# Image and vector field loaded ahead of weights and late gathers, VectorE's first step in an order of its own, attention masks of one head read four times

## What is computed

```python
# image filter, per image o (vf0, vf1: the vector field)
u = sigmoid(o / 0.5); q = 0
for _ in range(10):
    q = max(q - 0.5 * (rowdiff(u) * vf1 + coldiff(u) * vf0), 0)
    Tq = div(vf1 * q, vf0 * q)          # differences the other way
    u = sigmoid((o - Tq) / 0.5)
img = (o - Tq) / 0.5
# text
h = emb[tokens] + positions
for l in range(4):
    h = layernorm(h + attention(h, l)); h = layernorm(h + mlp(h, l))
# fusion on concat(img, h)
mask = (j <= i) & (j > i - 64)          # the same for all 8 heads
h = h + window_attention(layernorm(h), mask)
h = h + spikes(relu(layernorm(h) @ Wfc) ** 2 @ Wproj)
```

## Time and profile before

| | |
|---|---|
| median of 3 runs | 1001.82 us (1001.42 to 1001.96) |
| the profiled execution | 999.17 us, of which the span of its instructions is 997.3 us |
| busy in the span | PE 905.2 us (91%), DVE 834.9 (84%), ACT 699.3 (70%), POOL 122.3 (12%) |
| chain that ended last | DVE 47%, PE 25%, ACT 16%, issue 9%, DMA 2% |
| granted TensorE clock | 0.976 in the mean |

### The profile page before, as it was taken

One profiled execution on the slowest core, in us unless ns is written; L12 is line 12 of the kernel. 1 busy time (PEld: TensorE's weight loads), 2 busy tenths in 40 slices (PEclk: granted clock), 3 DMA queues, 4 the chain that ended last, 5 costly groups with the idle time before them and its releaser, 6 DMA issues.

```text
span 997.3 us, 18874 instructions
## 1 busy us (share of the span) xinstructions
PE 905.2 (91%) x6960; PEld 700.2 (70%) x6960; DVE 834.9 (84%) x1160; ACT 699.3 (70%) x2252; POOL 122.3 (12%) x147
## 2 busy tenths in 40 slices
PE   5489999999999999999999997889998999999997
PEld 4267777777777777777777775767675766667675
DVE  2999999999999999999999998987899599352443
ACT  2666876976877877877876875757767686767842
POOL 6201011011011011101101111101010111000000
PEclk9699999999999999999999999999998999999999
DMA  7311120031010121010220010000001000100000
GB/s 173 113 35 28 66 89 19 22 122 45 18 45 17 32 90 39 17 46 14 70 80 11 17 38 11 12 22 12 27 17 38 17 22 17 44 27 2 17 1 32
DMA packets 24925, 39.00 MB, mean 39 GB/s; under 512 B 4001, under 2 KB 20609, under 8 KB 23553
## 3 DMA queue, kind: packets, MB, share of 16 engines
q1 hardware_dynamic: 24448, 36.74, 11.6%
q0 software_dynamic: 384, 1.05, 0.5%
HBM read 22.21 MB, written 5.24 MB: 28 GB/s over the span
## 4 chain that ended last, share of the span: by engine, by line
DVE 47%; PE 25%; ACT 16%; issue 9%; DMA 2%; POOL 1%; SPq 0%; DVEq 0%; POOLq 0%; ACTq 0%
ACT prob L1086 7%; PE ps_t L849 7%; DVE f L1726 4%; DVE f L1753 4%; PE ps_m L860 4%; DVE f L1748 4%; DVE p L1738 4%; DVE f L1757 4%; DVE neg_max L1762 4%; DVE f L1743 3%; ACT u L1073 3%; DVE f L1721 2%; DVE f L1710 2%; PE ps_s L796 2%; DVE f L1699 2%
## 5 line engine op out<-in xcount | busy, mean ns | idle before, releaser
L1086 ACT ACTIVATE prob<-ps_s,neg_max 128x128 f32<-128x128 f32 x512 | 181.3, 408 | 7.3 <-DVE neg_max L1762 7.3
L1086 ACT ACTIVATION_READ_ACCUMULATOR prob<-ps_s,neg_max 128x1 f32 x512 | 126.6, 249 | 0.0
L655 PE MATMUL ps_t<-w,hidT 128*128 128x256 f32 x512 | 125.7, 383 | 0.0
L1094 ACT ACTIVATE probT<-ps_t 128x512 f32<-128x512 f32 x128 | 81.1, 634 | 44.3 <-PE ps_t L601 28.7
L655 PEld LDWEIGHTS ps_t<-w,hidT 128*128 128x128 f32 x512 | 91.1, 190 | 12.1 <-ACT hidT L1168 3.0
L849 PE MATMUL ps_t<-km,w_fc 128*128 128x384 f32 x256 | 93.9, 503 | 1.0 <-ACT km L1282 1.0
L601 PE MATMUL ps_t<-ident,prob 128*128 128x128 f32 x512 | 81.5, 283 | 12.9 <-ACT prob L1086 6.7
L601 PEld LDWEIGHTS ps_t<-ident,prob 128*128 128x128 f32 x512 | 60.0, 144 | 36.6 <-issue 14.7
L1762 DVE TENSOR_REDUCE neg_max<-ps_s 128x8 f32<-128x1024 f32 x64 | 77.5, 1211 | 4.6 <-PE ps_s L591 4.6
L1341 ACT ACTIVATE prob<-ps_s,neg_max 128x128 f32<-128x128 f32 x192 | 53.8, 376 | 22.6 <-DVE neg_max L1935 22.2
L849 PEld LDWEIGHTS ps_t<-km,w_fc 128*128 128x128 f32 x256 | 47.5, 195 | 26.8 <-issue 3.7
(11 more groups left out here) (179 smaller groups left out, 2038.9 us busy)
## 6 DMA issues: line engine op xcount, KB each, us to landing
w<-in_w SPq DMA_DIRECT2D x8, 1024.0 KB, 5.0
u<-u SPq DMA_DIRECT2D x80, 63.0 KB
p<-p SPq DMA_DIRECT2D x80, 63.0 KB
w_attn<-in_w_attn SPq DMA_DIRECT2D x4, 768.0 KB, 5.4
out<-w SPq DMA_DIRECT2D x7, 384.0 KB, 2.5
o_all<-in_o SPq DMA_DIRECT2D x4, 512.0 KB, 3.7
filtered<-f_out SPq DMA_DIRECT2D x4, 512.0 KB, 3.2
x<-filtered SPq DMA_DIRECT2D x8, 256.0 KB, 2.8
```

What stands on the lines that cost most here:

```text
L655: last = mm(ps_t[:, 0, D * t:D * t + D], hidT[:, m, P * t:P * t + P], w2[:, m], start=False, stop=(m == MC - 1), skip_group_check=True)
L1086: last = A(prob[:, n % 2, hh], ps_s[n % 2][:, hh], ACT.Exp, scale=-1.0, bias=neg_max[:, n % 2, hh:hh + 1], accum_out=den)
L1094: A(probT[:, 4 * half:4 * half + 4].rearrange("p h k -> p (h k)"), ps_t[:, 1], ACT.Copy).then_inc(s["act_pT"], 1)
```

## The change

1. SP issues the image right after the tokens, and the vector field (its column component, `vf[:, 1]`, first, with the semaphore `l_vf`; the row component with `l_vf_rows`) ahead of `w_attn`. Its wait before u<-u of iteration 0 is for eight of POOL's constants (`N_EARLY`) in place of nine.
2. POOL waits for `l_qkv` before it issues the six late gathers. The masks are built for one head: 256 columns to clear in place of 1024, and nine selections on 128 columns in place of 512. The readers take the 128 columns four times, through an access pattern that repeats them.
3. TensorE's 40 transposes at the start wait for eight constants in place of nine. ScalarE's first tanh waits for the constants, its program for `c_pool` at nine as before, and its first key copy for `c_heads` (`head_mask`).
4. VectorE does the first two filter operations before the positions; `head_max(0, 0)`, `(0, 1)` and `(0, 2)` come at other places of `first_step`; `pair_mask` is made between the iterations (`row_pairs`); `normalise(0, 0)` and `(0, 1)` stand before and after `divergence_rows(1)` and not after `divergence_out(1)`.

```diff
             sp.dma_start(tokens[:], d["tokens"]).then_inc(s["l_tok"], 16)
+            load_images(0).then_inc(s["l_img"], 16)
...
             sp.dma_start(pe[:], d["pe"]).then_inc(s["l_pe"], 16)
-            load_images(0).then_inc(s["l_img"], 16)
+            for comp, loaded in ((1, "l_vf"), (0, "l_vf_rows")):
+                for img in range(2):
+                    sp.dma_start(vf[64 * img:64 * img + 64, comp], ...).then_inc(s[loaded], 16)
             sp.dma_start(w_attn[:, :, 0:3 * D], d["w_attn"][0][:, :, 0:3 * D]).then_inc(s["l_qkv"], 16)
-            for img in range(2):
-                for comp in range(2):
-                    sp.dma_start(vf[64 * img:64 * img + 64, comp], ...).then_inc(s["l_vf"], 16)
...
-            sp.wait_ge(s["c_pool"], N_CONST)
+            sp.wait_ge(s["c_pool"], N_EARLY)
             rows_below(0)
             sp.wait_ge(s["g_emb"], 16 * (B - 2))
...
                 if b == 1:
                     const(pool.memset(v[:], 0.0))
                     assert c == N_CONST
+                    pool.wait_ge(s["l_qkv"], 16)
...
-                    const(pool.affine_select(out=m, in_=m, ..., pattern=[[0, 4], [1, P]], channel_multiplier=-1))
+                    const(pool.affine_select(out=m, in_=m, ..., pattern=[[1, P]], channel_multiplier=-1))
...
-                    last = A(quad[hb], mask[:, 0].rearrange("p a k -> p (a k)"), ACT.Copy)
+                    last = A(quad[hb].rearrange("p (a k) -> p a k", a=4), mask[:, 0].unsqueeze(1).to_broadcast([P, 4, P]), ACT.Copy)
```

More of the change, by code:

```diff
@@ L252, in build @@
         block = ctx.enter_context(nc.Block())
-        N_CONST = 8 + 1
+        N_EARLY = 8
+        N_CONST = N_EARLY + 1
         N_CONST_ALL = N_CONST + 2 + 9 + 3
@@ L416, in _ @@
             const(pool.memset(p1[:, 0], 0.0))
+            assert c == N_EARLY
             pool.wait_ge(s["c_idx"], 1)
@@ L785, in tile_scores @@
                     pe_.wait_ge(s["f_k"], n + 1)
-                    m = mask[:, 1].rearrange("p a k -> p (a k)")
+                    m = mask[:, 1].unsqueeze(1).to_broadcast([P, 4, P])
                     for hb in range(2):
-                        mm(quad[hb], ident_h[:], m, start=True, stop=False, skip_group_check=True)
+                        mm(quad[hb].rearrange("p (a k) -> p a k", a=4), ident_h[:], m, start=True, stop=False, skip_group_check=True)
                 for c in range(FKV):
@@ L1139, in keys_out @@
             def keys_out(k, g):
+                if k == 0:
+                    act.wait_ge(s["c_heads"], 1)
                 act.wait_ge(s[f"pe_k{g}"], k + 1)
@@ L1253, in first_step @@
                 queries_out(1)
+            act.wait_ge(s["c_pool"], N_EARLY)
             act.wait_ge(s["l_img"], 16)
@@ L1669, in _, with head_pairs, row_pairs, positions_first @@
                     dve.sem_inc(s["gen_free"], 1)
[L1671 to L1678, removed]
-            pe_rows = pe[:].unsqueeze(1)
-            dve.wait_ge(s["g_emb_first"], 32)
-            dve.wait_ge(s["l_pe"], 16)
-            tt(h[:, 0:2], h[:, 0:2], pe_rows.to_broadcast([P, 2, D]), ALU.add).then_inc(s["h_ready"], 1)
+            dve.wait_ge(s["c_pool"], N_EARLY)
+            pe_rows = pe[:].unsqueeze(1)
+            def head_pairs():
+                dve.tensor_reduce(head_mask[:], ident[:].rearrange("p (j o d) -> p o j d", o=2, d=TKD), AX.XY, ALU.add).then_inc(s["c_heads"], 1)
+            def row_pairs():
+                for r in range(4):
+                    tick(dve.tensor_reduce(row_mask[:, r:r + 1], ident[:, 32 * r:32 * r + 32], AX.X, ALU.add))
+                dve.wait_ge(s["chain"], chain[0])
+                link(tt(pair_mask[:], row_mask[:, 0:2], row_mask[:, 2:4], ALU.add))
+                ts(pair_mask[:], pair_mask[:], SCALE_F, None, ALU.mult).then_inc(s["c_scaled"], 1)
+                dve.wait_ge(s["c_scaled"], 1)
+            def positions_first():
+                dve.wait_ge(s["g_emb_first"], 32)
+                dve.wait_ge(s["l_pe"], 16)
+                tt(h[:, 0:2], h[:, 0:2], pe_rows.to_broadcast([P, 2, D]), ALU.add).then_inc(s["h_ready"], 1)
             def positions_rest():
@@ L1864, in first_step @@
             def first_step():
+                head_pairs()
                 columns_apart(0)
                 columns_weighed(0)
-                head_max(0, 0)
+                positions_first()
                 rows_apart(0)
@@ L1872, in first_step @@
                 flux_rows(0)
+                flux_cols(0)
+                head_max(0, 0)
+                divergence_columns(0)
                 head_max(0, 1)
-                flux_cols(0)
-                divergence_columns(0)
                 divergence_rows(0)
@@ L1878, in first_step @@
                 divergence_out(0)
-                head_max(0, 2)
+                row_pairs()
                 positions_rest()
                 columns_apart(1)
+                head_max(0, 2)
                 head_max(0, 3)
@@ L1892, in first_step @@
                 divergence_columns(1)
+                normalise(0, 0)
                 divergence_rows(1)
+                normalise(0, 1)
                 divergence_both(1)
                 divergence_out(1)
-                normalise(0, 0)
-                normalise(0, 1)
                 restart()
```

23 lines of the change are left out of this document (11 added, 12 removed).

## The result

The kernel got slower, by 0.9%: **1011.04 us** in the median of 5 runs (1008.13 to 1012.5), against 1001.82 for the kernel before on the same chip; ratio 1.0089, interval 1.0069 to 1.0108. The profiled execution has a span of 1009.3 us, 12.0 more than before.

The account below looks back on a forecast made before the run. The text phase was taken as one long DVE chain, timed by iteration 2's start: divergence_rows(0) at 37.3 plus 28.3 gives 65.6 against 59.57, +6.0 us, so 1007.8 us; range 1004 to 1011.5, with A and C 1002 to 1011.5.

Parts of the forecast that it names:

- First gathers at 13.5 to 14: Early loads: the first two gathers, no longer sharing with the third to the eighth, land then, against 16.1 before.
- l_qkv at 13.8: Early loads: w_attn complete at 13.8 us (11.5 to 15.5), after 2.75 MB at the old trace's rates.
- rival D: Late gathers beside busy DVE stretch when issued, up to 6 us more; +11 us, 1013 us; chance 0.08.
- Landing 5.0 us after the last start: Late gathers: the last starts at 20.3 and lands 5.0 us later, so all have landed at 25.3.
- G: End of SP's wait for the late gathers, where w_attn is issued; forecast at 25.3 us, against 19.8 before.
- Loads in order, then the halo: 12.0 us: SP's queue: w2 lands 11.6 us after the late-gather wait, then p<-p of iteration 0 takes 0.4 us.
- Rival A: SP's queue: p<-p overtakes the big loads; iteration 2 +0.9 to +2.9 us, some 1003.5 us; chance 0.10.
- B: Rival: halo overtakes and late gathers land 3 us after their start; 1.3 to 3 us faster, 999.7 us; chance 0.10.
- C: Rival: halo queues, but l_qkv at 12 and gathers landing in 3.5 us; +0.8 to +2.6 us, 1003.5 us; chance 0.12.
- T 37.3: Start of divergence_rows(0) on DVE, forecast at 37.3 us, 1.8 us later than before, after waiting some 10 us.
- Reciprocals copied at T + 22.7: TensorE and ScalarE chain: 8.3 us after the exponentials up to rden_out; DVE waits 3.3 us before the first normalise.
- or add one: TensorE's clock on the chain from exponentials to reciprocals: could take up to 2 us off, or add one.

Follow-up runs that it names:

- e_nowait: The changed kernel without POOL's wait for l_qkv before the late gathers; 1005.14 us, ratio 1.0014 to the kernel before.
- b_wait: The kernel before with only POOL's wait for l_qkv ahead of the late gathers added; 1002.96 us, ratio 0.9991 to the kernel before.
- e_halo_mid: The changed kernel with the first p<-p issued ahead of the w1 and w2 loads, still after the late gathers; 1003.35 us, ratio 1.0016 to the kernel before.
- e_max_early: The changed kernel with head_max(0, 2) directly after divergence_out(0), as before the change; 1010.56 us, ratio 1.0055 to the kernel before.
- e_norm_last: The changed kernel with both normalise after divergence_out(1), as before the change; 1008.43 us, ratio 1.0053 to the kernel before.
- b_mask: The kernel before with the mask part of the change alone; 1001.55 us, ratio 0.998 to the kernel before.
- e_combo_nowait: The changed kernel with the first p<-p ahead of SP's late-gather wait, both normalise after divergence_out(1), no POOL wait for l_qkv; 997.19 us, ratio 0.9953 to before.

## Why the prediction was right

The side and the mechanism came out: the halo behind the loads and the late gathers, the wait for the reciprocals, and then the old pace. The size was put too low, 6.0 us against 9.2, and what agrees is in part errors that cancel. Point by point, by its own steps:

- **First gathers at 13.5 to 14, tanh 1.4 us earlier.** The positions came at 13.77. The reason given, that the first two gathers no longer share with the other six, is not borne out: without the wait they came at 14.31 (`e_nowait`), and the wait alone brought 0.5 us (`b_wait`, 15.66 against 16.18). The rest came with the new order of the loads, which no run takes alone. The tanh was only 0.14 us earlier: the image had landed at 4.95, not 6.38, but ScalarE's table load (1.28 us), which ran at 0.79 before, now stood behind the wait for it, at 4.95. That can have cost at most the 0.94 us that DVE waited for u<-u at 15.39.
- **l_qkv at 13.8.** It was issued at 5.69 and landed 9.0 us later, at 14.7; the first late gather began 0.8 after that, at 15.46. Together 1.5 us more than the 14.0 of the sum. The working has a slip: 2.75 MB from 2.4 us on, at 0.319 MB/us until 9 and at 0.236 then, give 11.7 and not 12.9. Put right it would have missed by 1.2 us more.
- **head_max(0, 0) at about 22, DVE before divergence_rows(0) at 25.5.** 23.68 and 27.2, behind the six filter operations of the sum (the section on the change says five). TensorE's clock was granted at 0.66 from 16 to 20 us, where the scores are made. This was named, at some 5 us; it cost 1.4 (5.10 us for the 16 matmuls, 3.72 before), and as said it changed nothing, since DVE waited 12 us behind it.
- **Six gathers, 6.25 us from first to last start.** 23.25 less 15.46 is 7.79. The two first ones took 1.99 and 1.43 us, not 0.95. This was rival D, which I had at 8 chances in 100; it came true for 1.5 us of its "up to 6". The mis-sized term is the argument "a gather is mostly no SBUF reading". The sentence that before no gather ran beside a DVE instruction is not exact either: the third (8.13 to 9.08) ran beside the small ones of `row_mask` and `pair_mask`, and took 0.95.
- **Landing 5.0 us after the last start.** 3.6 (26.84). I had chosen the row of the gather (5.4, in a full machine) over that of a small transfer (3), and the truth lay nearer to the latter. This error cancelled about half of the first two, by luck: G at 26.86 against 25.3.
- **Loads in order, then the halo: 12.0 us.** 12.5. `e_halo_mid` shows that it is what stands ahead in the queue. "Cannot land before w2" is too strict, though: w2 landed 10.1 us after 29.58, at 39.7, and DVE had begun on p<-p at 39.36. Rival A, the halo that overtakes, is refuted, and B with it; C needed gathers at 22 or so, which `e_nowait` had (20.64; it came out 2.3 us late, within C's range) and the changed kernel had not.
- **T 37.3**: 39.36. **Exponentials done at T + 14.4**: the last one begins at 53.39 and takes 0.45, T + 14.5. **DVE at the first normalise at T + 19.4**: 63.02 less 4.25 is T + 19.4. **Reciprocals copied at T + 22.7**: 62.58 and 0.41, T + 23.6; the chain through TensorE and ScalarE took 9.15 us and not 8.3, so the wait was 4.25 and not 3.3. This chain goes with TensorE's clock: 8.11 us at a granted 0.78 (`e_max_early`), 8.3 at 0.76 (before), 8.55 at 0.73 (`e_halo_mid`, `e_nowait`; wait 3.65), 9.15 at 0.68 here, 9.38 at 0.66 (`e_norm_last`). In the 9 us ahead of it TensorE was busy for 2.2 of them here, at 0.50. It is the "or add one" that the prediction had named and not put into its sum.
- **Iteration 2 at 65.6, +6.0**: 68.43, +8.9. The 2.8 us are 1.56 at G, 0.5 in the loads and 0.77 behind T. The time was 9.2 us over and the forecast 6.0; it stands near the upper end of the range, for the same reason. That it is inside owes something to luck: the two terms that the range names, l_qkv at 15.5 and a landing of 5.4, give 1009.9 at most, and the 1011.5 was not worked out.
- **Masks: 0.** In the changed kernel 0, as said; in the kernel before they are worth 1.5 us of DVE (`b_mask`), which the prediction had not asked. (The longest of the nine selections took 1583 ns; 1432 is the longest of the line shown.)
- **The old pace from 60 us on.** Through the text phase SP's transfers of the same number are 8.9 us late at first and 8.2 at the end of it (623 us). In the fusion phase this becomes 11.8 by 754 us, and 12.0 after. The first step falls into one stretch; the kernel before, and the same work in the changed kernel, 8.2 us later:

```profile
630.00:640.00 10.00, 10.00 (x102) 8.83 (x101) 9.36 (x15) 8.07 (x23) 1.32 (x1) 0.92 0.04 13
```

```profile
638.20:648.20 10.00, 10.00 (x92) 8.75 (x93) 8.81 (x13) 7.04 (x20) 1.42 (x1) 0.74 0.04 13
```

TensorE is busy for all 10 us in both, but gets 92 matmuls through in place of 102, at a granted clock of 0.74 in place of 0.92. From the p<-p at 639.16 to the next u<-u the changed kernel takes 11.45 us, the kernel before 10.02. A second step of 1.1 us lies between 712 and 733 us, at a clock of 0.92 where it was 1.00. So dips of the granted clock fall in other places and cost more in this one execution. The medians show no such loss: less the start of iteration 2 they are 942.3 us before and 942.6 after. That these 3 us are the clock's and not the change's is argued from this, not shown by a run.

## What to carry to other kernels

When an engine is made earlier, look at once at what it will meet next: here one small transfer stood in a program, and in a queue, behind 2 MB of loads and a wait that it did not need, and this was invisible while the engine came late. A small transfer on which the busiest engine waits goes ahead of large ones on the same queue, and a wait placed in an issuing engine's program is paid by all that is issued after it. An in-order engine should also not be given an instruction that needs another engine's chain before work that is ready.

## What the hardware did that was not expected

**A gather that begins beside a VectorE instruction with two inputs in SBUF is held until that ends.** DVE and POOL of `e_combo_nowait`:

```profile
7.92 1.21 DVE L1705 TENSOR_TENSOR f<-u 128x1024 f32<-128x1024 f32 x1
9.24 1.23 DVE L1711 TENSOR_TENSOR f<-f,vf 128x1024 f32<-128x1024 f32 x1
```

```profile
8.13 1.83 POOL L424 DMA_INDIRECT h<-in_emb,tok_idx  x1 [0.27 <-POOL v L427]
10.27 1.01 POOL L424 DMA_INDIRECT h<-in_emb,tok_idx  x1 [0.30 <-issue]
```

The tensor-tensor operations end at 9.13 and 10.47, the gathers that began beside them at 9.96 and 11.28: 0.83 and 0.81 us later. In the changed kernel 16.62 and 18.36 are followed by 17.45 and 19.18. In all twelve traces every gather that began inside a tensor-tensor operation of 128x512 elements or more, with more than 0.13 us of it left, ended 0.81 to 0.84 us after it, and the others took 0.94 to 0.96 us, but for the first of a kernel (1.21 in each). It is the start that counts: the gather that began in `e_combo_nowait` at 14.09, ahead of the positions (14.33 to 15.02), took 0.94 us. Whether a scalar-tensor-tensor or a tensor-scalar holds a gather too is open: none began in the middle of one. I expected in `e_combo_nowait` just this, 0.8 us after the end.

The mask's selections show the same lock from both sides. POOL and DVE of `b_wait`:

```profile
28.14 0.90 POOL L436 TENSOR_SCALAR_AFFINE_SELECT mask<-mask 64x512 bf16<-64x512 bf16 x1
29.18 1.43 POOL L437 TENSOR_SCALAR_AFFINE_SELECT mask<-mask 64x512 bf16<-64x512 bf16 x1
30.75 1.43 POOL L436 TENSOR_SCALAR_AFFINE_SELECT mask<-mask 64x512 bf16<-64x512 bf16 x1
32.32 1.43 POOL L437 TENSOR_SCALAR_AFFINE_SELECT mask<-mask 64x512 bf16<-64x512 bf16 x1
33.89 0.63 POOL L439 TENSOR_SCALAR_AFFINE_SELECT mask<-mask 64x512 bf16<-64x512 bf16 x1
```

```profile
28.47 1.65 DVE L1711 TENSOR_TENSOR f<-f,vf 128x1024 f32<-128x1024 f32 x1
30.15 1.54 DVE L1727 TENSOR_TENSOR f<-f 128x1024 f32<-128x1024 f32 x1
31.72 1.53 DVE L1733 SCALAR_TENSOR_TENSOR p<-f,vf 128x1024 f32<-128x1024 f32 x1
33.18 1.21 DVE L1763 TENSOR_REDUCE neg_max<-ps_s 128x8 f32<-128x1024 f32 x1
```

The engines take turns. The selections of 1.43 us end at 30.61, 32.18 and 33.75, each 0.5 us after the DVE instruction that ran as it began (30.12, 31.69, 33.25); and these three DVE instructions end 1.07 or 1.08 us after the selection that ran as they began (29.04, 30.61, 32.18). Beside the maximum, which reads PSUM, a selection takes its own 0.63 us. The selection of 0.90 us ends at 29.04, 0.5 us after a tensor-scalar with one input (27.42 to 28.55), which took 1.13 us where it takes 0.69 in `b_mask`: that one takes part in the turns too. The Trainium skill (SBUF — State Buffer, "Who interferes with whom") calls the shared ports an exclusive lock and says that a VectorE instruction with two SBUF inputs contends with a GpSimd instruction that reads SBUF. The traces agree. It infers that a tensor-tensor operation leaves descriptor generation alone; here the gathers speak against that. A gather also reads its indices from SBUF, which may be the part that is held; no run separates the two.

**One queue serves large and small nearly in order.** p<-p (two transfers of 63 KB) landed 3.6 us after its issue with small loads ahead (`e_halo_mid`), and 8.3 and 8.5 us with 2 MB ahead (changed kernel, `e_nowait`). The order is not exact: in the changed kernel DVE began on p<-p at 39.36, and w2, ahead of it in the queue, had landed at 39.7. Whether a second queue would have let the small transfer past the loads is open: every run moved it within its own.
